# First-layer units of expert 0 made tile by tile, the first ahead of the second tile's transposes

## What is computed

```python
x = x + xattn(layernorm(x), ctx, ctx, Wq, bq, Wk, bk, Wv, bv)
xt = layernorm(x).reshape(4096, 256)
S = sigmoid(xt @ Wg).T                  # 8 experts
G, I = top_k(S, 1024)                   # each expert picks 1024 rows
ex = xt[I]
hid = gelu(einsum('ekh,ehf->ekf', ex, W1) + b1[:, None, :])      # 256 -> 1024
out = (einsum('ekf,efh->ekh', hid, W2) + b2[:, None, :]) * G[..., None]
x = x + zeros.at[I].add(out)
```

## Time and profile before

| what | value |
|---|---|
| median of 3 runs | 515.65 us (514.68 to 515.69) |
| profiled execution, time | 513.6 us |
| its span | 511.8 us |
| PE busy | 477.8 us, 93% of the span |
| VectorE, ScalarE, POOL busy | 335.9, 316.9, 292.6 us |
| TensorE's granted clock, mean | 0.968 |

### The profile page before, as it was taken

One profiled execution on the slowest core, in us unless ns is written; L12 is line 12 of the kernel. 1 busy time (PEld: TensorE's weight loads), 2 busy tenths in 40 slices (PEclk: granted clock), 3 DMA queues, 4 the chain that ended last, 5 costly groups with the idle time before them and its releaser, 6 DMA issues.

```text
span 511.8 us, 10700 instructions
## 1 busy us (share of the span) xinstructions
PE 477.8 (93%) x3807; PEld 345.5 (68%) x3807; DVE 335.9 (66%) x759; ACT 316.9 (62%) x607; POOL 292.6 (57%) x393
## 2 busy tenths in 40 slices
PE   7899999998338999999999999999999999999995
PEld 6688888877226458648747845864874784685484
DVE  6688999978983688675385466547538546535721
ACT  3877777866574781594396188359439618836920
POOL 2758999995306077456636726745662672673044
PEclk9999999999558999999999999999999999999999
DMA  7730866566802669449617817843772781673024
GB/s 232 238 101 1 242 170 165 148 184 187 235 1 75 172 160 133 86 135 138 133 33 200 168 21 196 165 52 128 142 135 56 185 158 22 188 105 41 1 33 50
DMA packets 91946, 64.21 MB, mean 125 GB/s; under 512 B 53060, under 2 KB 87816, under 8 KB 91912
## 3 DMA queue, kind: packets, MB, share of 16 engines
q1 hardware_dynamic: 78992, 46.41, 33.1%
q0 software_dynamic: 12288, 17.05, 20.9%
q10 hardware_dynamic: 632, 0.31, 0.2%
HBM read 35.83 MB, written 16.91 MB: 103 GB/s over the span
## 4 chain that ended last, share of the span: by engine, by line
PE 84%; DVE 7%; ACT 3%; issue 2%; DMA 2%; POOL 1%; POOLq 0%; SPq 0%; DVEq 0%; ACTq 0%
PE bank L1212 77%; PE bank L1219 3%; DVE cmp L928 2%; PE bank L1232 1%; PE bank L1508 1%; DMA ctx<-in_ctx 1%; ACT g L679 1%; DVE xres L1138 1%; DVE passed L938 1%; ACT xres L683 1%; DVE junk L978 1%; DMA ex<-rows_d,ids 1%; POOL yo L424 1%; DVE cnt L936 1%; DVE oneh L1084 0%
## 5 line engine op out<-in xcount | busy, mean ns | idle before, releaser
L1212 PE MATMUL bank<-w2h,xres 128*128 128x256 f16 x1024 | 169.3, 273 | 0.0
L1212 PE MATMUL bank<-exT,w1h 128*128 128x512 f16 (+1 forms) x528 | 152.9, 372 | 0.8 <-issue 0.8
L1212 PE MATMUL bank<-w2l,xres 128*128 128x256 f16 x512 | 139.6, 273 | 0.0
L513 POOL DMA_INDIRECT out<-yo,ids_s x64 | 101.5, 1586 | 48.3 <-ACT yo L699 27.7
L1138 DVE TENSOR_TENSOR xres<-g,xres 128x512 f16<-128x512 f32 x128 | 87.7, 690 | 53.2 <-ACT xres L683 43.6
L1212 PEld LDWEIGHTS bank<-w2h,xres 128*128 128x128 f16 x1024 | 99.9, 98 | 12.3
L699 ACT ACTIVATE yo<-yt,ge 128x256 f32<-128x256 f32 x63 | 32.0, 508 | 118.6 <-DVE yt L1166 96.0
L679 ACT ACTIVATE g<-bank,b1e 128x512 f32<-128x512 f32 x128 | 88.2, 689 | 18.2 <-PE bank L1212 12.0
L1212 PE MATMUL bank<-exT,w1l 128*128 128x512 f16 (+1 forms) x264 | 98.3, 372 | 0.0
L496 POOL DMA_INDIRECT ex<-rows_d,ids x64 | 67.2, 1050 | 41.2 <-DVE ids L1101 22.4
L1212 PEld LDWEIGHTS bank<-exT,w1h 128*128 128x128 f16 x528 | 50.9, 98 | 56.2 <-issue 1.0
(11 more groups left out here) (249 smaller groups left out, 776.8 us busy)
## 6 DMA issues: line engine op xcount, KB each, us to landing
w2r<-in_L_ffn_W SPq DMA_DIRECT2D x8, 1024.0 KB
w1r<-in_L_ffn_W SPq DMA_DIRECT2D x8, 1024.0 KB
xres<-in_x SPq DMA_DIRECT2D x8, 512.0 KB, 5.9
out<-xres SPq DMA_DIRECT2D x4, 1024.0 KB, 7.2
ctx<-in_ctx SPq DMA_DIRECT2D x7, 512.0 KB, 4.7
rows_d<-xrow SPq DMA_DIRECT2D x7, 512.0 KB, 3.5
b_bc<-in_L_ffn_b SPq DMA_DIRECT2D x8, 128.0 KB, 3.6
ex<-rows_d,ids POOLq DMA_INDIRECT x64, 3.1
```

Source lines behind the costliest of these rows:

```text
L513: pool.indirect_dma_start(out=rows_out, out_offset=bass.IndirectOffsetOnAxis(ap=ids_s[:, t:t + 1], axis=0), in_=yo[:, t, :], in_offset=Non ...
L1212: last = pe.matmul(out, lhs(a, c), rhs(b, c), start=i == 0, stop=i == len(terms) - 1)
```

## The change

Early units get a third argument, a tile. For the first half (tiles 0 and 1) each of the four units is made in two calls of 128 columns instead of one of 256. Unit 0 of tile 0 goes ahead of the transposes of tile 1, and `keep_awake` before it makes 5 matmuls instead of 8. The wait for ScalarE's copy of tile 0 now stands before that unit, the wait for VectorE's copy of tile 1 stands before the first call on tile 1.

```diff
-            def early_unit(f, q):
+            def early_unit(f, q, tile=None):
-                cols = slice(q * 256, (q + 1) * 256)
+                cols = slice(q * 256, (q + 1) * 256) if tile is None else slice(tile * P, (tile + 1) * P)
...
             row_transposes(0)
-            keep_awake(D_[:, 1, 0:2 * P], order16[:, 0:2].rearrange("p a k -> p (a k)"), 8)
-            row_transposes(1)
+            keep_awake(D_[:, 1, 0:2 * P], order16[:, 0:2].rearrange("p a k -> p (a k)"), 5)
             pe.wait_ge(s["w1_lo_s"], 4)
             pe.wait_ge(s["ex0_act"], 1)
+            early_unit(0, 0, 0)
+            row_transposes(1)
+            for f in range(1, EARLY):
+                early_unit(f, 0, 0)
             pe.wait_ge(s["ex0_dve"], 1)
-            early_unit(0, 0)
+            early_unit(0, 0, 1)
             row_transposes(2)
-            early_unit(1, 0)
+            early_unit(1, 0, 1)
+            early_unit(2, 0, 1)
             row_transposes(3)
-            for f in range(2, EARLY):
-                early_unit(f, 0)
+            early_unit(3, 0, 1)
             list_of(1, False)
```

## The result

The changed kernel takes 516.23 us (median of 20 runs, 514.80 to 518.37), the kernel before 515.14 beside it (20 runs, 514.01 to 515.91). The ratio is 1.0020 with a 95% interval of 1.0011 to 1.0029, so the change costs 1.1 us, at the edge of the 0.2% that I had called no change and on its slower side. I had forecast 0.1 us less. The time lies inside my wide range of 513.8 to 516.6 and just outside the forecast's own, 515.0 to 516.05.

The account below looks back on a forecast made before the run. TensorE was taken as the path to the first gelu; a filled wait of 0.39 less added transposes and matmul time gave 0.09 us, so 515.65 - 0.1, rounded to 515.5 us. Own range 515.0 to 516.05, wide range 513.8 to 516.6.

Parts of the forecast that it names:

- Where the first unit starts: Unit 0 on TensorE starts at 161.32 us as before, since it still waits for ScalarE's copy of tile 0.
- TensorE's work up to the list: From unit 0 to expert 1's list: 3.38 us instead of 3.47, so the list starts 0.09 us earlier.
- the wait of 0.39 in front of tile 2: TensorE's idle time before tile 2's transposes in the old order, 0.39 us, goes because small matmuls fill it.
- The removed fillers, "worth 0": Three `keep_awake` matmuls dropped ahead of unit 0, about 0.1 us each, ended before a wait, so worth 0.
- rival 2: Longer idle time on TensorE ahead of unit 0 brings the clock down: +1.7 - 0.1, so 517.2 us; chance 0.10.
- VectorE: Copy of tile 1 comes 1.55 us later, one-hot pieces end at 165.06, tile 3's copy about 165.40; just in time.
- Rival 4: VectorE's last one-hot piece or copy of tile 3 comes late and replaces the removed wait: +0.3, 515.9 us; chance 0.06.
- The stop, "taken unchanged": Unexplained gaps in expert 1's list on TensorE, 1.67 us lost, stay the same; bounded between 0 and twice that.
- The end follows the first gelu: Second half of unit 0 and ScalarE's first gelu starting x earlier should bring the kernel's end x earlier.
- The cap by SP's transposes: SP's transposes of tiles 4 to 7 start at 168.08 regardless of TensorE; unit 8 needs them, limiting larger gains.
- Rival 1: The new order loses the gaps in expert 1's list: 1.8 us off, 513.85 us; chance 0.18.
- Rival 3: Weight loads of 0.10 us bound the 48 small matmuls on TensorE: +2.1, so 517.6 us; chance 0.04.

Follow-up runs that it names:

- a_third: The changed kernel unaltered, run again in a group with the stop: 515.74 us, ratio to before 1.0007 [0.9995, 1.0019].
- a_hold: The changed kernel with the gathers of tiles 4 to 7 held back until unit 0's second half is done: 522.74 us, one run.
- b_hold2: The kernel before with the gathers of tiles 4 to 7 held back until unit 0's second half is done: 523.0 us, one run.
- a_fourth: The changed kernel unaltered, run again in another group with the stop: 515.88 us, ratio to before 1.0021 [1.0008, 1.0034].
- b_list_in: The kernel before with a semaphore per gather of tiles 4 to 7 and expert 1's list behind the early units' second halves: 514.33 us, ratio 0.9984.
- a_list_in: a_best with expert 1's list moved behind the early units' second halves, in a group with the stop: 516.85 us, ratio to before 1.0025.
- a_fill12b: The changed kernel with 12 `keep_awake` matmuls instead of 5 ahead of unit 0, in a group with the stop: 516.80 us, ratio to before 1.0025.
- a_best2: a_best repeated in a group with the stop: 516.23 us, ratio to before 1.0027 [1.0015, 1.0039].
- a_swap: The changed kernel with copies of tiles 0 and 2 on VectorE, 1 and 3 on ScalarE, without the stop: 512.65 us, ratio to before 0.9989.
- b_fill_mid: The kernel before with seven more filler matmuls behind tile 1's transposes, in a group without the stop: 513.02 us, ratio to before 0.9986.
- a_best: a_swap with a semaphore for each gather of tiles 4 to 7, in a group without the stop: 512.12 us, ratio to before 0.9966.
- a_again: The changed kernel unaltered, in a group without the stop: 513.39 us against 513.31, ratio to before 0.9987 [0.9969, 1.0004].
- b_again: The kernel before unaltered, run again in a group with the stop: 515.78 us, ratio to before 1.0005 [0.9993, 1.0018].
- b_fill5: The kernel before with 5 `keep_awake` matmuls instead of 8, in a group without the stop: 514.27 us, ratio to before 1.0007.

## Why the prediction was wrong, step by step

*Where the first unit starts.* Right: 161.32 in both kernels, behind ScalarE's copy.

*TensorE's work up to the list.* Right wherever the clock was up. In a_third 24 of the small matmuls took 163.48 - 162.14 = 1.34, 0.056 each, as I had taken it; a_hold took 3.35 where the sum gave 3.38. Since the old order without the stop took 3.32 in b_hold2, the wait of 0.39 in front of tile 2 that I had counted as a gain was only 162.47 - 161.57 - 6 x 0.109 = 0.25 there. At half clock, as in after, the pace is 0.107.

*The removed fillers, "worth 0".* Wrong for the clock, and it is rival 2, to which I gave 0.10. The idle time in front of unit 0 was 1.42 in after and 1.58 in a_fourth, and the clock fell at its end or just behind it. It didn't with 1.46 in a_third and 1.44 in a_hold, so the fall may come here or not. But the fall isn't what decided the 1.1 us. After and a_fourth, with it, have their first gelu at 13.64 and 13.79; a_third, without it, at 14.04. And among after's executions those with a higher mean clock are not quicker to match: 516.09 (11) against 516.38 (9) at 0.962 and less, and in a_third's group 516.33 (7) against 515.38 (5). So far as these traces tell, time that the clock takes before the stop ends is hidden by the stop.

*VectorE.* The one-hot pieces came 0.5 later than forecast (163.02 instead of 162.53), since the transposes in front ran at half clock. In a_hold, without the stop and at full clock, they were made in time, the list ran in one piece and the second half followed. Rival 4 didn't come.

*The stop, "taken unchanged".* This is the step that failed, and it carried the sign. I had read it as 1.67 us lost in the list, a fixed length that would move with the list. By the runs it ends 11.5 to 11.8 us behind the first gather's issue in nine of ten traces, whatever the order (11.02 in b_list_in, where the last wait is for VectorE). In before, one matmul of the list was left at that moment; in after five matmuls of a unit, and the whole list: 168.50 - 167.37 = 1.13 up to the second half, against 167.29 - 167.22 = 0.07. The difference, 1.06, is nearly all of the 1.21; the other 0.15 is the later end, since the first gather was issued 0.13 later. The list was not the only thing left: the copies of tiles 2 and 3 ended at 168.11 and 168.09, so without it the second halves would have started some 0.3 earlier and no more (an estimate from a_list_in, whose TensorE went on 0.05 behind its copy). I had bounded the stop between nothing and twice its size, which gave the range its width, but had no rival in which the same stop is paid by other work. (Its upper end, 516.05, is 515.65 + 0.4; counted from the forecast of 515.5 the spread of +0.4 gives 515.9.) With the gathers held the two orders lie 0.08 apart at the first gelu (10.75 and 10.83), and in the group without the stop after isn't shown to be slower; so the cost needs the stop.

*Why more is left at its end* is only half shown. The stop begins earlier with the small matmuls: at 7.2 to 8.3 in a_third, a_fill12b, a_best2 and a_list_in, against 8.8 to 9.8 in the four traces of the old order. Only at half clock does it begin as late (9.8 and 10.3), and then the half clock has used the time. So either way after's order reached the end of the stop with a unit and a list to go.

*The end follows the first gelu.* Right: 343.6 behind it in both profiles, and so in every trace whose clock held and whose unit 8 didn't wait, to some 1 us. The cap by SP's transposes was real too, at a first gelu of 166.1 (a_swap) and 167.1 (b_fill_mid).

*Rival 1, the stop goes.* It went in two of five groups, for every kernel alike, so not by the order of TensorE. There the ratio was 0.9987 and not the 1.8 us off that I had given it, because before loses its stop as well.

*Rival 3, weight loads.* Out. 48 matmuls of 128 columns, each with its own load, ran in a_third and a_hold, those of a stretch without gaps 0.056 apart. The Trainium skill (TensorE: Matmul & The Clock Gate, section Back-to-back issue gap) gives some 81 ns for such a stream; the traces don't bear it out here, and decide.

*What stays open.* What the stop is. It needs the gathers of tiles 4 to 7 at that time (it is gone in b_hold2 and a_hold, one run each), it ends some 0.5 us before the last of their rows are signalled (167.71 in before's trace), and some groups of runs don't have it though the gathers are issued at the same times. In none of the ten traces that have it does a packet of the instruction queues fall into it, so nothing there speaks for instruction fetch. One rival was never tested, and the lost semaphore events speak for taking it seriously: the recording itself. Every execution of the five groups comes with a span and a granted clock, so none is known to have run unrecorded; small matmuls are more instructions to record in the same time, which would fit an earlier stop. Whether recording holds TensorE up, or both suffer from one thing beside the gathers, is open, and with it whether the change costs anything in an execution that nobody records. Which resource TensorE and the gathers share, and why the order by tiles runs into it earlier, no run here shows. Nor is a version shown that is quicker than before in both kinds of group: a_best is in the one (-0.34%) and not in the other (+0.27%), b_list_in was run only with the stop (-0.16%).

## What to carry to other kernels

A wait that the profile doesn't explain must not be carried into a forecast as a constant: ask whether its length or its end is fixed, for with a fixed end the cost of a change is what it moves behind that end, and gains made in front of it are nothing. Put the small work that others wait for last (here the list) where it isn't in front of them when such a wait ends. When one consumer is served earlier, look at once for the next one's source, here SP's transposes, before the gain is booked. And compare a version in more than one group of runs: a_best would have been taken for the better kernel by the group in which it ran first. Before a gap without a cause is put down to the kernel, count whether the trace still holds the events that it should: here about three in ten of the semaphore events of DMAs were missing in every trace with the gap.

## What I had not expected of the hardware

- TensorE issued one to four small matmuls at a time, with 0.5 to 1.3 us from one such group to the next, on and off for up to 4.3 us (a_fill12b, whose first gap is a wait for a late copy) while gathers ran. Most of these gaps have no releaser in the traces. The completion of transposes reached ScalarE and VectorE 1.3 us (tile 1 in a_fill12b) to 5.4 us (tile 2 in a_list_in) behind their issue instead of 0.43 to 0.53. It came and went between groups of runs, and the time of the kernel before went with it by 1.9 us.
- Where this happens, some 1200 to 1500 of 4300 semaphore events of DMAs are missing from the trace, from the first gathers on (before: 3 of 16 on record for tile 3's gather; a_again: 16).
- The clock came up behind the threshold search anywhere between 156.90 (b_again) and 166.49 us (b_fill5) in kernels that have nearly the same work up to there, and fell again behind 1.4 to 1.6 us of idle in two of four traces. It fell near the end of the stop or behind it in five of ten (at 11.4 to 13.4 in the table).
